# Edge rows of a graph kernel padded to 129 columns, and loaded batch by batch

## What is computed

```python
row = edge_index[0]                                        # src, one node per edge, in no order
edge_aggr = jnp.zeros((n, HIDDEN)).at[row].add(edge_features)
global_expand = jnp.repeat(global_feat, reps, axis=0)
combined = jnp.concatenate([x, edge_aggr, global_expand], axis=-1) @ W_c + b_c
h = jax.nn.softplus(combined @ W1 + b1)
h = jax.nn.softplus(h @ W2 + b2)
x = _layernorm(x + h @ W3 + b3)
```

## Time and profile before

| | us |
|---|---|
| time, median of 3 runs | 2049.62 (2043.18 to 2053.18) |
| the profiled execution, its own time | 2046.89 |
| its span, first to last instruction | 2044.3 |
| PE busy in the span | 1830.6 (90%) |
| mean granted TensorE clock | 0.944 of full |

### The profile page before, as it was taken

The page is one execution under the profiler, slowest core; times in us unless marked ns, Lnnn a source line. Parts: engine busy times, 40 slices in busy tenths (PEclk is TensorE's granted clock), DMA queues, the critical chain, the costliest instruction groups (busy, mean ns, idle before and its releaser), DMA issues.

```text
span 2044.3 us, 61300 instructions
## 1 busy us (share of the span) xinstructions
PE 1830.6 (90%) x14853; PEld 1708.0 (84%) x14853; DVE 1311.6 (64%) x3881; ACT 1040.2 (51%) x3479; POOL 1167.6 (57%) x1482
## 2 busy tenths in 40 slices
PE   7888898888898888888898989888988999999996
PEld 4788888888888888888888888788888999999973
DVE  7755555555555555555556656556555988988966
ACT  1434443344344443444444444344445888888886
POOL 1565656665656565566655665566564555555545
PEclk9898898998899999999999999999998999999998
DMA  6498767767666565665666566666557999999942
GB/s 138 156 271 274 214 189 206 202 189 205 205 182 182 172 174 159 172 174 168 176 184 174 168 171 182 168 173 177 170 171 218 302 299 302 297 301 300 299 143 61
DMA packets 346502, 412.37 MB, mean 202 GB/s; under 512 B 28533, under 2 KB 249893, under 8 KB 344248
## 3 DMA queue, kind: packets, MB, share of 16 engines
q1 hardware_dynamic: 284176, 233.87, 39.5%
q0 software_dynamic: 54608, 174.58, 27.9%
q10 hardware_dynamic: 7689, 3.60, 1.0%
HBM read 233.69 MB, written 178.23 MB: 201 GB/s over the span
## 4 chain that ended last, share of the span: by engine, by line
PE 81%; issue 8%; DVE 3%; DMA 1%; another core or an unknown queue 1%; ACT 1%; POOL 0%; DVEq 0%; SPq 0%; ACTq 0%; POOLq 0%
PE ps L1228 55%; PE ps L1300 19%; PE ps L1186 2%; PE ps L1199 2%; PE ps L1190 1%; DMA members<-buckets 1%; DVE arena L802 1%; DVE arena L874 1%; PE ps L1335 1%; PE ps L1196 1%; PE ps L1238 1%; DVE hotc L640 0%; DVE xn L884 0%; DVE stats L890 0%
## 5 line engine op out<-in xcount | busy, mean ns | idle before, releaser
L1228 PE MATMUL ps<-arena 128*120 128x129 f32 x9084 | 1223.2, 290 | 111.7 <-issue 103.0
L1228 PEld LDWEIGHTS ps<-arena 128*120 128x120 f32 x9084 | 1139.3, 193 | 142.9 <-issue 132.3
L521 POOL DMA_INDIRECT buckets<-arena,index x757 | 777.6, 1027 | 553.0 <-ACT arena L1013 320.8
L802 DVE TENSOR_SCALAR arena<-slot_no,slot_f 128x360 f32<-128x360 f16 x1514 | 549.6, 415 | 595.6 <-PE ps L1228 321.7
L1013 ACT ACTIVATE arena<-ps 120x387 f32<-120x387 f32 x757 | 372.6, 493 | 865.2 <-PE ps L1228 520.1
L1300 PE MATMUL ps<-mark,members 128*128 128x128 f32 x3648 | 413.6, 276 | 6.5 <-ACT mark L1114 4.1
L1300 PEld LDWEIGHTS ps<-mark,members 128*128 128x128 f32 x3648 | 410.9, 193 | 9.3 <-issue 7.3
L846 DVE TENSOR_SCALAR mark<-node_no,members 128x128 f32<-128x128 f16 x1368 | 360.3, 330 | 60.8 <-DMA members<-buckets 52.8
L563 POOL TENSOR_TENSOR sums<-sums,staged 128x128 f32 x456 | 225.0, 493 | 199.5 <-POOL sums L563 110.1
L967 ACT ACTIVATE reach<-block_no,arena 128x120 f16<-128x120 f16 x806 | 313.0, 390 | 0.9 <-PE ps L1238 0.7
L1108 ACT ACTIVATE apart<-node_no,members 128x128 f32<-128x128 f16 x456 | 181.0, 397 | 32.0 <-DMA members<-buckets 24.0
(11 more groups left out here) (169 smaller groups left out, 616.5 us busy)
## 6 DMA issues: line engine op xcount, KB each, us to landing
members<-buckets SPq DMA_DIRECT2D x456, 258.0 KB, 3.6
arena<-in_feats SPq DMA_DIRECT2D x201, 512.0 KB
buckets<-arena,index POOLq DMA_INDIRECT x757
xn<-in_x ACTq DMA_DIRECT2D x1, 2800.0 KB
arena<-in_xT SPq DMA_DIRECT2D x11, 250.0 KB, 4.0
out_rows<-xn SPq DMA_DIRECT2D x11, 224.0 KB
buckets<-arena,direct_at POOLq DMA_INDIRECT x98
arena<-in_src SPq DMA_DIRECT2D x1, 805.5 KB
```

The lines of the kernel that those rows point to most:

```text
L521: pool.indirect_dma_start(units, bass.IndirectOffsetOnAxis(ap=index[0:SLOTS, s, b:b + 1], axis=0), rows[0:SLOTS, o, :], None).then_inc(sca ...
L802: dve.tensor_scalar(perm[0:TP, b, t, :], slot_no[0:TP, :, :].rearrange("p r b -> p (r b)"), slot_f[0:TP, s, b * TPB + t:b * TPB + t + 1], ...
L1228: mm = pe.matmul(ps[0:SLOTS, MOVED + b, r * ROWF:(r + 1) * ROWF], perm[0:TP, b, t, r * SLOTS:(r + 1) * SLOTS], feat[0:TP, s, b * TPB + t, ...
```

## The change

- The host hands over the edge features with a 129th column of zeros, so a partition's rows lie in DRAM as they lie in `feat`.
- `load` brings one batch (2 tiles, 258 words, 1032 bytes per partition, in one piece) instead of one chunk (8 pieces of 512 bytes per partition). A load is issued as soon as the batch that had its place in the body before has been moved; only the load of batch 15 waits for `direct_landed`. The waits of a load on earlier loads go.
- `feats_loaded` becomes four semaphores, one per place; each counts 64 for a full chunk.
- Because the load now writes column 128 too (zeros), `set_locals` has to come after it: ACT waits for the chunk's four loads where it waited for the free place.

```diff
-    feats_v = feats[0:COLS * TP, :].rearrange("(p t) f -> p t f", t=COLS)
+    feats_v = feats[0:COLS * TP, :].rearrange("(p t) f -> p (t f)", t=COLS)
...
-        feats_loaded = [sem(f"feats_loaded{s}") for s in range(2)]
+        feats_loaded = [sem(f"feats_loaded{s}") for s in range(XS)]
...
-            def load(c, s, turn):
-                wait(sp, feats_loaded[s % 2], turn * 16)
-                sp.dma_start(feat[0:TP, s, :, 0:D], feats_v[:, bass.ds(c * (CB * TPB), CB * TPB), :])\
-                  .then_inc(feats_loaded[s % 2], 16)
+            def load(c, s, b):
+
+                n = TPB * ROWF
+                sp.dma_start(feat[0:TP, s, b * TPB:(b + 1) * TPB, :].rearrange("p t f -> p (t f)"),
+                             feats_v[:, bass.ds(c * (CB * n) + b * n, n)]).then_inc(feats_loaded[s], 16)
...
             def reload(i, s):
-                if s == XS - 1:
-                    sp.wait_ge(direct_landed, i * (16 * TPB))
-                else:
-                    sp.wait_ge(moved, packed(i, (s + 1 - XS) * CB))
-                load(i * XS + s, s, i * (XS // 2) + s // 2)
+                for b in range(CB):
+                    if s * CB + b == BODY - 1:
+                        sp.wait_ge(direct_landed, i * (16 * TPB))
+                    else:
+                        sp.wait_ge(moved, packed(i, s * CB + b + 1 - BODY))
+                    load(i * XS + s, s, b)
...
             def set_locals(i, s):
                 c = i * XS + s
-                if s % XS == XS - 1:
-                    wait(act, direct_landed, (i + s // XS) * (16 * TPB))
-                else:
-                    wait(act, moved, packed(i, (s + 1 - XS) * CB))
+                act.wait_ge(feats_loaded[s % XS], (i + s // XS) * (16 * CB) + (16 if isinstance(i, int) and c == CHUNKS - 1 else 16 * CB))
+                if isinstance(i, int) and c == CHUNKS - 1:
+                    act.wait_ge(rest_loaded, 16)
...
             def move(i, k):
                 c, s, b = i * XS + k // CB, k // CB % XS, k % CB
                 if b == 0:
-                    pe.wait_ge(feats_loaded[s % 2], (i * (XS // 2) + k // CB // 2) * 16 + 16)
+                    pe.wait_ge(feats_loaded[s], (i + k // CB // XS) * (16 * CB) + (16 if isinstance(i, int) and c == CHUNKS - 1 else 16 * CB))
...
-        "src": inputs["src"], "feats": inputs["edge_attr_128"],
+        "src": inputs["src"], "feats": np.pad(np.asarray(inputs["edge_attr_128"]), ((0, 0), (0, 1))),
```

More of the change, by code:

```diff
@@ L377, in _ @@
               .then_inc(ids_loaded, 16)
-            def load(c, s, turn):
-                wait(sp, feats_loaded[s % 2], turn * 16)
-                sp.dma_start(feat[0:TP, s, :, 0:D], feats_v[:, bass.ds(c * (CB * TPB), CB * TPB), :])\
-                  .then_inc(feats_loaded[s % 2], 16)
+            def load(c, s, b):
+                n = TPB * ROWF
+                sp.dma_start(feat[0:TP, s, b * TPB:(b + 1) * TPB, :].rearrange("p t f -> p (t f)"),
+                             feats_v[:, bass.ds(c * (CB * n) + b * n, n)]).then_inc(feats_loaded[s], 16)
             for s in range(XS):
-                load(s, s, s // 2)
+                for b in range(CB):
+                    load(s, s, b)
             sp.wait_ge(zeros_set, 1)
@@ L408, in _ @@
                 if c < CHUNKS - 1:
-                    load(c, c % XS, c // 2)
+                    for b in range(CB):
+                        load(c, c % XS, b)
             s, n = c % XS, (NBAT - c * CB) * TPB - 1
-            sp.wait_ge(feats_loaded[s % 2], c // 2 * 16)
-            sp.dma_start(feat[0:REST, s, n, 0:D], feats[COLS * TP:E, :]).then_inc(rest_loaded, 16)
-            sp.dma_start(feat[0:TP, s, 0:n, 0:D], feats_v[:, COLS - n:COLS, :]).then_inc(feats_loaded[s % 2], 16)
+            sp.dma_start(feat[0:REST, s, n, :], feats[COLS * TP:E, :]).then_inc(rest_loaded, 16)
+            sp.dma_start(feat[0:TP, s, 0:n, :].rearrange("p t f -> p (t f)"), feats_v[:, (COLS - n) * ROWF:COLS * ROWF])\
+              .then_inc(feats_loaded[s], 16)
             for o in range(STREAMS):
```

## The result

The change makes the kernel slower by 0.77%.

What follows compares the result with a forecast made beforehand. PE was taken to bound the kernel, with 227 us of stage 2's idle time and lower clock all there was to win. Every term was 0, so 2046.89 + 0 = 2046.9, forecast as 2046 us, range 1996 to 2076.

Steps and rivals of the forecast that it cites:

- The bound: PE in stage 2's loops, busy 89%; 147 us idle and 80 us lost to clock, 227 us to win; stage 3 untouched.
- SP: "costs nothing": SP's queue: 16 loads per body for 4, 0.5 us each, 8 us of about 29, hidden; cost 0.
- DMA engines: Feature loads: 55 ns per 1032-byte packet, share falling from 27.2% to 24.5%; not the bound, so 0 on the path.
- Rival D: Feature loads: the change doesn't save packets, share and time stay; shares the forecast's chance of 0.38.
- ACT: "costs 0": ACT's column write: its wait moves from place free to chunk loaded, ending before ACT arrives; cost 0.
- The margin of 2.5 us: ACT's column at the fourth place: the load's wait ends 2.5 us or more before ACT arrives, in the worst body.
- B: Rival, slower: ACT's wait for the load takes hold at the fourth place, 24 to 48 us, 2070 to 2095; chance 0.11.
- The stalls: "0": PE's stalls behind the direct scatters: they stand without loads, so the change in loads adds or saves 0.
- A: Rival, faster: the burst of loads feeds PE's stall, smaller bursts win 29 to 58 us, about 2016 us; chance 0.36.
- C: Rival, slower: steadier loads, batches 12 to 14 earlier, lengthen PE's stalls by 0.5 us per body, 24 us, 2070; chance 0.15.

Runs made afterwards that it cites:

- e2: Changed kernel with rows of 512 bytes unpadded, one load per batch still issued early, ACT's old wait: 1.0035 of the kernel before.
- e13: Kernel before plus 588 DMAs from SP, each 4 bytes on each of 128 partitions, into a scratch nobody reads: 1.0048 of the kernel before.
- e14: Kernel before plus 588 DMAs from SP, each 4 bytes on one partition, into a scratch nobody reads: 1.0050 of the kernel before.
- e8: Changed kernel with unpadded 512-byte rows, ACT's old wait, and a chunk's four loads issued together at the old moment: 1.0054 of the kernel before.
- e4: Changed kernel with the four loads of a chunk issued together once the whole place is free: 1.0061 of the kernel before.
- e1: Kernel before with padded rows, one load per chunk in 4128-byte pieces, ACT's column write behind it: 1.0006 of the kernel before.
- e3: Kernel before with only ACT's wait changed, column written after the chunk's load has landed: 1.0040 of the kernel before.
- e9: Kernel before without direct batches, the sixteenth batch of each body moved like the others: 1970.40 us, 0.9606 of the kernel before.
- e10: Kernel before with padded rows, one load per chunk, and ACT's column written one batch later: 1.0004 of the kernel before.
- e7: The changed kernel run again, unaltered, against the kernel before: 1.0066.
- e5: Kernel before without direct batches, on the chip where the kernel before took 1779.21 us: 1802.15 us, 1.0127 of the kernel before.

## Why the prediction was wrong

**The bound** was read rightly. PE bounds, stage 3 is untouched, and the whole difference is idle time and lower clock in the loops (18.2 of 17.8 us, within reading).

**SP: "costs nothing" is the step that failed.** I counted 16 issues of 0.5 us, saw that SP has nothing else to do, and wrote 0. SP's own time is indeed hidden. But the number of loads had no term for what it does to the others, and that is the main part of the loss: 603 more at 12 ns (e2), 17 ns (e13, e14) or 18 ns (e8) are 7 to 11 us. No row of the trace before shows that price; a lower and an upper bound for it were missing, where the stalls were priced only by whether loads are in flight. What the runs showed in place of 0: the four loads for one cost 11.1 us [8.0, 14.3] with no byte, no piece and no moment changed (e8), and 588 DMAs of 4 bytes cost 9.8 and 10.2 us.

**DMA engines: wrong size, no consequence.** I took 55 ns for a packet of 1032 bytes, between two measured sizes, and a share of 24.5%. The share is 27.9%, and a piece of 1032 bytes took 65 ns, above even the 61 ns that I had as the dear end. The 16 small packets of each load are not the reason: e8 has as many and its loads cost no more per MB than before's. In e8's loops the row is

```profile
q1 hardware_dynamic: 196230, 94.61, 26.3%
```

which is 26.3% x 21440 / 94.61 = 59.6 us per MB. The pieces of e4, issued in bursts, took 62 ns each (5682 / 91136), on another chip, so 3 ns of the 65 may come with the spread. The far end of the line, 2064 bytes, comes from another stage; with the pieces of e1 as the far end, 24.7% x 21440 / 22656 = 234 ns for 4128 bytes, the line gives 60 ns. Whether the rest lies in where the pieces start is not shown. In e1 the share did fall, and the time stayed, so "0 on the path" holds. Rival D's outcome (nothing saved) came by another way: the packets were saved and their time wasn't.

**ACT: "costs 0" is wrong by some 2 us.** The margin of 2.5 us was read in the loops, and it holds there. It doesn't hold in the first bodies, where POOL's queue with its fills takes 85.5% of the DMA engines' time while the loads are due, and the last load of the fourth place takes up to 11.5 us to land, where I had 3.3 to 4.0. B named this condition and this place (a load behind POOL's writes while the engines are full), but put it into every second body instead of four. With 6.0 us of waits at e3's rate it is an estimated 2.4 us.

**The stalls: "0" is wrong.** The reason given, that a stall stands without loads too, is true and doesn't bear the conclusion. That loads are not needed for a stall doesn't say that more of them leave it as it was. By the pages of e8 and e14, PE is idle 220.7 and 218.2 us of the span for 213.7 before, and busy 1838.5 and 1835.7 us with the same matmuls for 1830.6; e13's profiled execution, its fastest of eight, shows no more idle time (212.1 us), only the late steps of `moved`. Two readings were wrong too. The stall of the earlier trace rows began before the two loads of the earlier trace rows, so these rows don't speak for A. And a stall isn't bound to the direct scatter: ACT waits for "remote" 83 times in 49 bodies, and 86 times in e9, which has no direct scatter.

**The rivals.** A, faster, is refuted: an eighth of the packets (e1, e10: 1.0006, 1.0004) gave nothing back, and smaller bursts (e2: 1.0035) didn't either. C had the direction and the number of completions right, "five completions fall into it instead of two", but its mechanism, batches 12 to 14 leaving earlier, falls with e4 and e8, and its price of 24 us was too high. B is real and small.

The parts are 7 to 11 us for the number and 2.4 us for ACT's wait, together 10 to 14 us, against 15.8 [10.4, 21.1] in the case's runs and 13.5 [8.2, 18.6] in e7. They meet; a few microseconds may be left that no run assigns.

## What to carry to other kernels

In a kernel whose bounding engine stalls without a visible wait, a further DMA isn't free, even where its issuing engine and the DMA engines have time to spare: count DMAs, and price a further one by adding some that carry a few bytes, which takes one run. Before splitting a load that is already hidden, ask what the finer pieces could win; here PE had waited for a load once, for 0.6 us, so the only thing that the split could do was to add. Look at the engines that wait for a result, and not only at the rows of the one that makes it: PE's rows showed 147 us of gaps, and hid that ACT waited about six microseconds for batches that they have as done. And take a covering margin from the worst stretch, the start of the loops with its one-time writes included, not from the steady part.

## What the runs showed of the hardware

- The same program of the kernel before took 1779.21, 2046.64, 2047.09, 2050.49 and 2077.20 us, each a median in one comparison on one chip, while its runs there lie within 5 to 17 us. On the fastest chip PE has no stall without direct batches: 0.1 us of idle time before 9672 matmuls (e5), where the same program has 73.7 us on another chip (e9). What differs between the chips the profiles don't tell. It decides what is worth doing: the direct batches gain 1.3% there (e5) and lose 3.9% on another chip (e9).
- A DMA of 4 bytes from SP, with nobody waiting for it, costs about 17 ns of the whole kernel's time on a chip with stalls (e13, e14).
- On the chips with stalls the step of a semaphore behind PE's matmuls comes late: the median moved batch has 1.0 us from the end of PE's row to the step of `moved` in the kernel before and 1.2 us with the change, and 13 ns in e5. The longest are over 7 us.
- Two indirect scatters of 128 rows each straight from the loads' buffer, once in a body, widen the distance between the chips by about 100 us: it is 268 us with them and 168 without. By two traces they don't make the stalls more (83 waits of ACT with them, 86 without), but longer (303.5 and 248.4 us in all).
- Halving the number of packets from 512-byte ones to 1032-byte ones left the DMA time per MB as it was (62.9 us for 60.8 when spread, 60.5 for 60.9 in bursts); pieces of 4128 bytes lowered it to 56.3.
